# Expert tiles: the next tile's high and low parts in the second chunk, ahead of the second weight copy and the rest of the product

## What is computed

```python
logits = x @ router_weight.T + router_bias
topk_logits, topk_idx = jax.lax.top_k(logits, TOP_K)          # 4 of 8
topk_w = jax.nn.softmax(topk_logits)
...
gate_up = jnp.einsum('nd,ejd->nej', x, gate_up_proj) + gate_up_proj_bias
gate, up = jnp.split(gate_up, 2, axis=-1)
gate = jnp.minimum(gate, SWIGLU_LIMIT)
up = jnp.clip(up, -SWIGLU_LIMIT, SWIGLU_LIMIT)
act = (up + 1.0) * gate * jax.nn.sigmoid(SWIGLU_ALPHA * gate)
out = jnp.einsum('nei,edi->ned', act, down_proj) + down_proj_bias
y = jnp.einsum('ned,ne->nd', out, combine)
```

## Time and profile before

| | us |
|---|---|
| median of 3 runs | 1552.16 |
| lowest, highest | 1545.53, 1553.2 |
| profiled execution | 1547.26 |
| its span, first to last instruction | 1545.4 |

### The profile page before, as it was taken

One profiled execution on the slowest core, in us unless ns is written; L12 is line 12 of the kernel. 1 busy time (PEld: TensorE's weight loads), 2 busy tenths in 40 slices (PEclk: granted clock), 3 DMA queues, 4 the chain that ended last, 5 costly groups with the idle time before them and its releaser, 6 DMA issues. The chain is left out here.

```text
span 1545.4 us, 18406 instructions
## 1 busy us (share of the span) xinstructions
PE 1084.3 (70%) x5074; PEld 741.6 (48%) x5074; DVE 1246.1 (81%) x1555; ACT 844.1 (55%) x1353; POOL 1025.6 (66%) x593
## 2 busy tenths in 40 slices
PE   5547575683837557233319999999999999999960
PEld 2112131231313122111218888888888888888850
DVE  1698999999998999998227888888888888888863
ACT  3464555464554556432117666666666666666644
POOL 0345557777676777678654777777777777777782
PEclk9777777675867768565559999999999999999995
DMA  1999998989878888894383555555555555555537
GB/s 64 244 274 253 258 258 232 259 242 262 238 233 232 238 261 230 253 246 129 106 303 116 146 147 144 144 147 147 148 143 151 152 151 150 152 150 144 151 42 224
DMA packets 137418, 292.22 MB, mean 189 GB/s; under 512 B 14880, under 2 KB 50464, under 8 KB 132640
## 3 DMA queue, kind: packets, MB, share of 16 engines
q1 hardware_dynamic: 97824, 242.48, 52.3%
q0 software_dynamic: 26880, 36.72, 14.3%
q10 hardware_dynamic: 12672, 12.58, 2.6%
HBM read 232.71 MB, written 59.02 MB: 189 GB/s over the span
## 5 line engine op out<-in xcount | busy, mean ns | idle before, releaser
L951 POOL TENSOR_TENSOR read<-state,c_rep 128x1024 f32<-128x1024 f32 x128 | 301.7, 2357 | 247.8 <-DVE state L791 240.0
L791 DVE TENSOR_TENSOR_SCAN state<-decay,p_bu 128x1024 f32<-128x1024 f32 x128 | 292.3, 2283 | 9.4 <-ACT decay L632 3.5
L632 ACT ACTIVATE decay<-first_wl,scan_rate 128x511 f32<-128x511 f32 x192 | 127.9, 713 | 249.7 <-DVE state L791 212.7
L1359 POOL DMA_INDIRECT total<-o_v,tok x144 | 228.0, 1583 | 40.0 <-issue 40.0
L479 PE MATMUL p_y<-read,small 128*32 128x512 f32 x512 | 96.0, 833 | 210.0 <-POOL read L951 210.0
L1304 DVE TENSOR_TENSOR al<-a_v,ah 128x512 fp32r<-128x512 f32 x144 | 209.5, 1455 | 41.6 <-ACT ah L1236 38.4
L1298 DVE TENSOR_SCALAR up_v<-up_v 128x512 f32<-128x512 f32 x144 | 155.5, 1080 | 77.1 <-ACT up_v L1229 75.1
L1236 ACT ACTIVATE ah<-a_v 128x512 fp32r<-128x512 f32 x144 | 91.6, 636 | 193.9 <-DVE a_v L1309 193.9
L394 POOL TENSOR_TENSOR first_wl<-first_raw,first_wh 128x2048 fp32r<-128x2048 f32 (+1 forms) x38 | 144.4, 3800 | 76.1 <-ACT first_wh L387 73.6
L394 POOL TENSOR_TENSOR wl<-raw_w,wh 128x2048 fp32r<-128x2048 f32 (+1 forms) x36 | 136.8, 3799 | 85.0 <-ACT wh L387 85.0
L782 DVE TENSOR_TENSOR p_bu<-first_wh,p_b 128x1024 f32<-128x1024 f32 x96 | 118.0, 1229 | 30.7 <-DMA first_wh<-scan_in 15.7
(11 more groups left out here) (200 smaller groups left out, 2992.5 us busy)
## 6 DMA issues: line engine op xcount, KB each, us to landing
first_wl<-scan_in SPq DMA_DIRECT2D x192, 256.0 KB
first_wh<-scan_in SPq DMA_DIRECT2D x192, 256.0 KB
first_raw<-in_w_experts SPq DMA_DIRECT2D x19, 1668.0 KB
raw_w<-in_w_experts SPq DMA_DIRECT2D x18, 1668.0 KB, 6.9
dt_rep<-scan_in SPq DMA_DIRECT2D x64, 256.0 KB
u_rep<-scan_in SPq DMA_DIRECT2D x64, 256.0 KB
first_rows<-queues SPq DMA_DIRECT2D x19, 544.0 KB, 6.9
xq<-queues SPq DMA_DIRECT2D x18, 544.0 KB, 6.9
```

Source lines behind the costliest of these rows:

```text
L632: act.activation(decay[t % 2][:, i, 1:LEN], dt_rep[t % RING][:, i, 1:LEN], ACT.Exp, scale=rate[:, g:g + 1])\
L791: dve.tensor_tensor_scan(flat(state[t % 4][:, :, :]), flat(decay[t % 2][:, :, :]), p_bu[:, :], 0.0, ALU.mult, ALU.add).then_inc(s_state, 1)
L951: pool.tensor_tensor(read[quad % 2][:, tiles[0]:tiles[0] + 2, :], state[t % 4][:, :, :], c_rep[s.p][:, :].unsqueeze(1).broadcast_to([P, 2, ...
L1359: pool.indirect_dma_start(total, bass.IndirectOffsetOnAxis(ap=tok[t.p][:, a:a + 1], axis=0), o_v[t.p][:, a, :], None, compute_op=ALU.add). ...
```

## The change

In ScalarE's order, the copies `xh` of the next tile (`copy_tile`, both halves) stand ahead of weight copy 1 instead of behind it, in the same chunk 1. In VectorE's order, the two subtractions that make `xl` (`rest_of_tile`) move from chunk 2 to chunk 1, where they stand behind the reading of the output before and ahead of `rest_of_product` of chunk 1. No instruction is added or taken away, and no semaphore or buffer changes.

```diff
@@ act_stage2
                 read_up(t, i)
                 if i == 0:
                     copy_share(t, expert)
-                if i < 2:
-                    copy_weights(act, t.at(1), i)
+                if i == 0:
+                    copy_weights(act, t.at(1), 0)
                 if i == 1:
                     for k in range(KD):
                         copy_tile(t.at(1), k)
+                    copy_weights(act, t.at(1), 1)
                 if i == 2 and later:
                     weigh_output(t.at(-1))
@@ dve_stage2
                 if i == 1 and later:
                     read_output(t.at(-1))
-                if i == 2:
+                if i == 1:
                     for k in range(KD):
                         rest_of_tile(t.at(1), k)
```

## The result

| | before | after |
|---|---|---|
| median of the runs taken together, us | 1553.2 (5 runs) | 1579.43 (5 runs) |
| profiled execution, us | 1547.26 | 1577.64 |
| its span, us | 1545.4 | 1575.8 |

The ratio is 1.0181, with a 95% interval of 1.0157 to 1.0205: the change makes the kernel 1.8% slower, some 28 us, where 17 (1.1%) were forecast. The sign and the mechanism held. The measured median, 1579.43, lies inside the range given for 8 in 10 (1556 to 1588) but above the forecast's own (1561 to 1577). The second figure leaves out the 5.5 us by which the traces differ ahead of the expert stage.

What follows compares the result with a forecast made beforehand. A closed ring of GpSimd, VectorE and ScalarE was taken to bound the expert stage; +0.48 us a steady tile (+15.8 over 33) and early intervals gave +17.0, from 1552.16 to 1569.2 us; own range 1561 to 1577, 8-in-10 range 1556 to 1588.

Steps and rivals of the forecast that it cites:

- The ring: Expert stage: GpSimd, VectorE and ScalarE wait on each other in a closed loop without TensorE, 19.01 us a tile.
- Item 1: ScalarE: two `xh` copies ahead of the second weight copy, for which GpSimd waits, add 0.95 us a tile (0.95 to 1.08).
- Item 2: VectorE: `xl`, one operand in PSUM, runs unheld beside GpSimd's gate/up weights; its 1.28 us are hidden.
- Item 3: TensorE: down product at E + 0.70, next tile at E + 2.20 instead of E + 3.05, 0.85 us earlier.
- E: End of GpSimd's operation for the low part of the gate/up weights; times in a tile count from it.
- Item 4: VectorE, chunk 0: clip at E + 6.66, 0.77 ahead of GpSimd's down weights, gets through; product is held; gains 0.47 us.
- The ring's own length: Steady expert tile, summed as 10.42 + 3.48 + 0.95 + 4.64 = 19.49 us against 19.01.
- The third interval: Early expert stage, 818.52 to 836.46 before: hangs on TensorE, which starts 0.95 - 0.85 later, +0.10 us.
- Rival A: VectorE, chunk 0: the clip is held too, 19.96 us a tile, +32.6, 1584.8 us; chance 0.15.
- Rival B: VectorE, chunk 0: the product gets through too, TensorE releases the loop, 18.19 us a tile, 1526 us; chance 0.11.

Runs made afterwards that it cites:

- before_wait: Kernel before, with GpSimd made to wait for the product of chunk 0 ahead of the low part of the down weights; 1517.85 us against 1550.02.
- before_short: Kernel before, with GpSimd making the low part of only 64 of 1024 down-weight columns in the loop (work left out); 1520.82 us against 1549.2.
- after_wait: The whole change, plus a GpSimd wait for the product of chunk 0 ahead of the low part of the down weights; 1520.15 us against 1549.2.
- dve_only: Kernel before with only VectorE's half of the change, `xl` moved to chunk 1; 1552.46 us against 1550.02.
- xh_chunk0_wait: Kernel before with `xh` in chunk 0, `xl` in chunk 1 and GpSimd's wait ahead of the down weights; 1536.65 us against 1549.2.
- after_filled: The changed kernel plus one VectorE operation of some 1.25 us, result unused, ahead of `al` of chunk 2; 1566.64 us against 1550.05 for the kernel before.
- after_bias: The changed kernel with VectorE's three bias copies moved from chunk 3 to behind `al` of chunk 2; 1577.13 us against 1552.36 for the kernel before.
- xh_chunk0: Kernel before with the `xh` copies in chunk 0, behind weight copy 0, and `xl` in chunk 1; 1542.55 us against 1550.02.
- tok_with_al: Kernel before with `xh` in chunk 0, `xl` then the token copy ahead of `al` in chunk 1, and GpSimd's wait; 1506.56 us against 1550.05.

## Why the prediction came out as it did

- **The ring as the bound**: right, and shown from three sides: a wait that opens it (before_wait), an operation cut short (before_short), and the same order at no cost once it is open (after_wait).
- **Item 1, the two copies on the ring**: right. 0.95 forecast; ScalarE's half alone gives 19.94 against a steady 19.01, +0.93.
- **Item 2, `xl` free beside GpSimd**: right, 1.28 for two. The row of `o_v` was the right one to take. What the Trainium skill ("SBUF — State Buffer", section "SBUF: two separate sides") says of two SBUF inputs agrees: `al`, which has them, is held, `xl` is not.
- **Item 3, TensorE starts earlier against E**: right. No wait for `xl` is left, the down product starts at E + 0.69 (0.70 forecast), and the next tile at E + 2.17 (2.20).
- **Item 4, clip through, product held**: right in 32 tiles of 34. The clip came at E + 6.74 (6.66 forecast), but 0.91 ahead of GpSimd's down weights, not 0.77, because these came 0.2 later, behind the longer scatter-add.
- **The ring's own length was mis-sized**: E to the end of the down weights was taken over from before at 10.42 and became 10.63. The term that was mis-sized is the first of the sum: item 2 priced `xl` where it goes, and the place that it leaves at nothing. Without it `al` of the third chunk starts 0.44 earlier, and a scatter-add beside it grows by 0.2. 33 x 0.19 (19.68 against 19.49) = 6.3 us of the missing 7.9.
- **The third interval, +0.10 forecast, +1.7 measured**: TensorE had stood still for 2.3 us ahead of a down product, and the granted clock behind it was 0.57, near the lower of its two levels (1.2 and 2.4 GHz), as the windows below show; the matmuls of the down product start 0.21 us apart there, where 0.12 is usual, and the next tile starts at E + 3.38. That is 1.2 of the missing 1.6; the rest wasn't traced. In two later tiles a dip came again (0.75 in the second window below, 0.64 from 1440 to 1444), TensorE reached chunk 0 late, and the clip was held: 20.16 instead of 19.68, +1.0 in all. The kernel before shows a granted clock of 1.00 in its windows of this stage; it has two tiles with late scatter-adds instead, 1.3, which the sum had left out on both sides. So the steady tiles miss 6.3 + 1.0 - 1.3 = 6.0, the third interval 1.6, the others 0.3.
- **Rival A** didn't come, but its 32.6 is nearer to the 28 (or 26.2) us than the forecast's 17 is. By the time alone A would have looked as good; what tells them apart is the clip at 0.43 and the wait of 4.46. That the time fell into the 8-in-10 range is owed in part to its reaching up over A.
- **Rival B** didn't come either. Its price for such a tile was right: 18.14 in after_wait against 18.19. What it left out is the copy of the tokens: in tiles shorter still (17.2 in dve_only, 17.7 in xh_chunk0_wait), a late scatter-add is followed by tiles of 20.2.

The pause, and windows of the changed kernel (busy us by engine, then TensorE's granted clock):

```profile
830.08 0.54 PE L1191 MATMUL p_o<-first_wh,ah 128*128 128x256 f32 x1 [2.31 <-DVE al L1305]
```

```profile
830.00:834.00 4.00, 3.92 (x16) 3.75 (x17) 2.78 (x6) 2.73 (x4) 0.16 (x1) 0.57 0.00 0
1364.00:1368.00 4.00, 4.00 (x18) 3.21 (x18) 2.43 (x6) 2.21 (x4) 3.39 (x3) 0.75 0.56 66
```

## What to carry to other kernels

Where a busy engine shows a wait, first look for a closed ring of other engines with the same period: TensorE was 95% busy and waited for `xl`, and making `xl` earlier cost 28 us, because the copies that were moved up with it stood on the ring. When two engines hold each other up, price every moved instruction twice, for itself and for what it shifts into or out of the other engine's way; an operation of four columns in the wrong place was held for 4.6 us and made the tile 19.6 us instead of 17.7, and a wait on the engine in the way gained 32 us in all. What is held anyway is a free place: put there what might be held, and keep ahead of it what isn't.

## What the runs showed of the hardware that was not expected

- A VectorE operation that starts first isn't safe. In the changed kernel the product began 0.43 to 0.45 us ahead of GpSimd's recorded start and was held for 3.98. The Trainium skill ("SBUF — State Buffer", section "SBUF: two separate sides") says that whoever starts first keeps the ports; going by recorded starts these rows don't agree. Whether GpSimd takes the ports before its recorded start is open; its down weights stand right behind a scatter-add here and are recorded as starting 0.56 before that one is over (1112.60 against 1113.16). Where they waited for the product instead, in most tiles of before_wait, they took 2.39 and not 2.99, so some 0.6 us of the recorded time are probably no work of their own.
- A scatter-add of 1.56 us can grow to 1.78, and a clip from 0.47 to 0.70, by what VectorE does 0.4 us earlier or later ahead of them (after_filled against after_bias).
- A pause of TensorE of 2.3 us was followed by a granted clock of 0.57, while the same kernel's regular pauses of 1.8 us left it at 1.00 in all but two tiles. The length of the pause alone doesn't decide: at the same place, behind the stage's second weight operation, xh_chunk0 paused for 1.86 us and fell to 0.50, and tok_with_al paused for 1.95 us and stayed at 1.00.
